# Softplus of a selective scan's steps: one function table, sums on TensorE, clamped integers in bf16, one store semaphore for each pair of buffers

## The chip, the core and the metric

The kernel runs on one core of a Trainium2 chip. The time is device microseconds for one execution. The kernel before takes 3646.77 us, the median of three runs (3645.39 to 3648.1). The work is spread over TensorE (PE in the profile), VectorE (DVE), ScalarE (ACT), GpSimd (POOL) and the DMA queues that SyncE (SP) issues to. The engines wait for each other through semaphores that the kernel sets by hand.

## The reference

Six layers follow each other on four sequences of 512 tokens of width 512: a quantized state-space layer, a cross-attention, a sparse mixture of experts, a self-attention, another cross-attention and another mixture. The change is in the first. What matters of it:

```python
dt8 = qa(dt_q @ dwq.T * (S_DTLN * dws), S_DT)      # round, clip to -128..127
dt = jax.nn.softplus(jnp.swapaxes(dt8, 1, 2) * S_DT + dt_bias[None, :, None])
u = u_q * S_U
A = -jnp.exp(A_log)
ys = ssm_scan(u, dt, A, B_q * S_B, C_q * S_C)      # needs dt and dt * u
```

So for each of 1024 channels and 4 x 512 tokens a product is rounded and clipped to an integer, scaled, a bias of the channel is added, and softplus of it, `dt`, and `dt * u` go to the scan.

## The kernel before

The kernel is a chain of sections, each ended by a barrier of all engines. The section here is `softplus` (L897 to L1007); ahead of it stands `x_proj`, behind it `scan`. It works on blocks of one sequence each (`NB` = 4, index `b`). A block is 8 tiles of 128 channels x 512 tokens, taken in pairs (`PAIRS` = 4, index `i`), so that an instruction mostly covers 128x1024 elements. The buffers `v` and `e` (f32) exist twice, for even and odd blocks, `w` once. The stages of a pair:

- products (L943, TensorE): two bf16 matmuls into PSUM `dps`, which has room for four pairs.
- rounding (L955, ScalarE): scale and add the constant MAGIC, which leaves an integer in the low bits; into `v`.
- clamping (L987, L988, VectorE): clip, then subtract MAGIC and multiply by the step, in place.
- bias (L965, ScalarE): one instruction for each tile, in place in `v`.
- Abs and Exp (L969, L972, ScalarE): e = exp(-|v|), into `e`.
- loss (L995, L996, VectorE): w = e - ((e + 1) - 1), what rounding loses of e when 1 is added.
- Ln (L977, ScalarE): e = ln(1 + e).
- steps (L1002, L1003, L1006, VectorE): w = e + w; v = max(v, 0) + w, which is dt; e = v * u.
- stores (L927, L929, SyncE): dt and dt * u to DRAM, two DMAs of 512 KB for a pair.

The order on each engine is that of its program. ScalarE goes through a block stage by stage: bias, Abs, Exp for the four pairs, then the rounding of the next block, then Ln. VectorE does four losses, clamps the next block, and then does four steps. A buffer `v` or `e` of a block may be written again when all eight stores of the block two before have landed; one semaphore for each half (`s_st[b % 2]`) counts them, and the first rounding of the block waits for it. Exp and Ln lie in different function tables, so the compiler puts a table load (ACT_TABLE_LOAD) ahead of each Exp stage and each Ln stage. SyncE fills `bc` at the head of the section with 32 broadcasts for the scan, and GpSimd works off a chain of small gathers and scatters (`add_cells`) beside all this. The section ends when the stores have landed and GpSimd is done.

Of the kernel before, what the change touches and what calls it, by code (L numbers as in the profile page):

```python
# [291 lines left out]
def mamba(nc, A, x_dram, xa, u, gate, owq, dtq, zero, rmw, soft, sgd, bcd, kv, gqk, ident, identb):  # L292
    with ExitStack() as ctx:
# [27 lines left out]
        softplus(nc, xa, u, dtq, dwq, dtb, kk, soft, bcd, rmw)  # L321
# [575 lines left out]
def softplus(nc, xa, u, dtq, dwq, dtb, kk, soft, bcd, rmw):  # L897
    with ExitStack() as ctx:
# [6 lines left out]
        dps = ctx.enter_context(nc.psum_tensor("sf_ps", [P, 4, 2, S], F32))  # L905
        bc = xa[:].rearrange("p j c -> p (j c)").bitcast(BF16).rearrange("p (m s) -> p m s", s=S)
        dtd, dud = soft
        with section(nc, "sf_mm", "sf_rnd", "sf_t", "sf_v", "sf_av", "sf_e", "sf_c", "sf_ln", "sf_dt", "sf_du", "sf_own",
                     "sf_bc", "sf_sum", "sf_st0", "sf_st1") as (
                block, s_mm, s_rnd, s_t, s_v, s_av, s_e, s_c, s_ln, s_dt, s_du, s_own, s_bc, s_sum, *s_st):  # L910
# [8 lines left out]
            @block.sync  # L919
            def _(sp):  # L920
                for m in range(2 * NS):
                    sp.dma_start(bc[:, m, :], bcd[m, 0:S].partition_broadcast(P)).then_inc(s_bc, 16)
                for b in range(NB):
                    for i in range(PAIRS):
                        n, k = b * PAIRS + i, b * CT + 2 * i
                        sp.wait_ge(s_dt, n + 1)
                        sp.dma_start(dtd[k:k + 2].rearrange("k p s -> p k s"), two(v, b, i)).then_inc(s_st[b % 2], 16)  # L927
                        sp.wait_ge(s_du, n + 1)
                        sp.dma_start(dud[k:k + 2].rearrange("k p s -> p k s"), two(e, b, i)).then_inc(s_st[b % 2], 16)  # L929
                sp.wait_ge(s_bc, 32 * NS)  # L930
                for s_half in s_st:
                    sp.wait_ge(s_half, 32 * PAIRS * (NB // 2))

            @block.tensor
            def _(pe):
                for b in range(NB):
                    for i in range(PAIRS):
                        n = b * PAIRS + i
                        if n >= 4:
                            pe.wait_ge(s_rnd, n - 3)  # L940
                        for h in range(2):
                            j = 2 * i + h
                            ins = pe.matmul(dps[:, n % 4, h, :], dwq[:, j * P:(j + 1) * P], dtq[:, b * S:(b + 1) * S],  # L943
                                            start=True, stop=True)
                        ins.then_inc(s_mm, 1)

            @block.scalar
            def _(act):
                def rounded(b):
                    for i in range(PAIRS):  # L950
                        n = b * PAIRS + i
                        act.wait_ge(s_mm, n + 1)
                        if b >= 2 and i == 0:
                            act.wait_ge(s_st[b % 2], 32 * PAIRS * (b // 2))
                        act.activation(two(v, b, i), dps[:, n % 4], ACT.Copy, scale=kk[:, W_DT:W_DT + 1],  # L955
                                       bias=MAGIC).then_inc(s_rnd, 1)

                rounded(0)
                for b in range(NB):
                    for i in range(PAIRS):  # L960
                        n = b * PAIRS + i
                        act.wait_ge(s_t, n + 1)
                        for h in range(2):
                            j = 2 * i + h
                            ins = act.activation(v[:, b % 2, j, :], v[:, b % 2, j, :], ACT.Identity, bias=dtb[:, j:j + 1])  # L965
                        ins.then_inc(s_v, 1)
# [13 lines left out]
            def _(dve):  # L980
                own = Order(dve, s_own)

                def clamped(b):
                    for i in range(PAIRS):
                        x = two(v, b, i)
                        dve.wait_ge(s_rnd, b * PAIRS + i + 1)
                        own.after(dve.tensor_scalar(x, x, MAGIC - 128.0, MAGIC + 127.0, ALU.max, ALU.min))  # L987
                        dve.tensor_scalar(x, x, MAGIC, S_DT, ALU.subtract, ALU.mult).then_inc(s_t, 1)  # L988

                clamped(0)  # L990
                for b in range(NB):
                    for i in range(PAIRS):
                        c = w[:, 2 * i:2 * i + 2, :]
                        dve.wait_ge(s_e, b * PAIRS + i + 1)
                        own.after(dve.tensor_scalar(c, two(e, b, i), 1.0, -1.0, ALU.add, ALU.add))  # L995
                        dve.tensor_tensor(c, two(e, b, i), c, ALU.subtract).then_inc(s_c, 1)  # L996
                    if b + 1 < NB:
                        clamped(b + 1)
                    for i in range(PAIRS):
                        n, c = b * PAIRS + i, w[:, 2 * i:2 * i + 2, :]  # L1000
                        dve.wait_ge(s_ln, n + 1)
                        own.after(dve.tensor_tensor(c, two(e, b, i), c, ALU.add))  # L1002
                        dve.scalar_tensor_tensor(out=two(v, b, i), in0=two(v, b, i), scalar=0.0, in1=c, op0=ALU.max,  # L1003
                                                 op1=ALU.add).then_inc(s_dt, 1)
                        dve.wait_ge(s_dt, n + 1)
                        dve.tensor_tensor(two(e, b, i), two(v, b, i), u[:, 2 * i:2 * i + 2, b * S:(b + 1) * S],  # L1006
                                          ALU.mult).then_inc(s_du, 1)  # L1007
# [1942 lines left out]
```

## Time and profile before

| | |
|---|---|
| median of 3 runs | 3646.77 us |
| profiled execution | 3662.09 us |
| its span, first to last instruction | 3660.3 us |
| TensorE, VectorE, ScalarE, GpSimd busy over the span | 88%, 66%, 48%, 33% |
| softplus, first product to VectorE's last operation | 266.64 to 387.39 us |
| table loads in softplus | 8, of 1283 ns each |

The numbers of the profile come from one execution with the profiler on; its own time is a little above the median of the runs. Busy times are shares of one engine, and a busy engine is only the bound where others wait for it. For a section this short the timeline says more than the busy share: start, length, and in brackets how long the engine had been idle before an instruction and what ended that. Matmuls overlap in the records, so their rate is read from their starts or from a sum over many. The granted clock of TensorE is a share of 2.4 GHz.

### The profile page before, as it was taken

The page shows a single profiled execution, that of the slowest core. Times are in us where ns is not written, and L with a number is a line of the kernel's source. Part 1 is how long each engine was busy: PE and PEld are TensorE (multiplying, and loading weights), DVE is VectorE, ACT ScalarE, POOL GpSimd, SP SyncE. Part 2 cuts the span into 40 slices and gives each one's busy share as a digit, 9 for nine tenths or more (in the row PEclk, how much of TensorE's full clock was granted, in tenths as well). Part 3 has the DMA queues.
Part 4 walks back from the last instruction along what each step waited for, and adds up shares of the span by engine and source line. Part 5 has one row for each costly group of instructions (what it writes and reads, how often), then busy time and mean ns, then how long its engine had stood idle before and what let it go on. Part 6 is the DMA issues. An engine that isn't in the chain of part 4 may idle for free. (4 is left out here: it accounts for less than half of the span.)

```text
span 3660.3 us, 34737 instructions
## 1 busy us (share of the span) xinstructions
PE 3219.4 (88%) x11045; PEld 1571.0 (43%) x11045; DVE 2431.8 (66%) x4472; ACT 1773.1 (48%) x3342; POOL 1203.4 (33%) x963
## 2 busy tenths in 40 slices
PE   3750699999999799999999999899899978999963
PEld 3330244444444345555455555344444444444432
DVE  8768899999999555555555555543421266999754
ACT  4748466666666334343434343344310125888621
POOL 0323699999999001010000000021388020000024
PEclk9975799999999899999999999999999997999977
DMA  7115425353432222222211111243622011000056
GB/s 258 48 60 166 149 93 147 100 138 101 124 112 75 99 74 67 69 78 66 70 52 52 61 55 52 95 139 123 231 106 98 0 64 58 1 1 1 1 162 212
DMA packets 201318, 334.67 MB, mean 91 GB/s; under 512 B 25648, under 2 KB 76208, under 8 KB 198064
## 3 DMA queue, kind: packets, MB, share of 16 engines
q1 hardware_dynamic: 187904, 298.69, 25.0%
q0 software_dynamic: 12208, 33.57, 3.3%
q8 instruction: 89, 1.46, 0.2%
q14 instruction: 93, 0.76, 0.1%
q10 hardware_dynamic: 1024, 0.20, 0.0%
HBM read 217.69 MB, written 114.69 MB: 91 GB/s over the span
## 5 line engine op out<-in xcount | busy, mean ns | idle before, releaser
L1282 POOL TENSOR_TENSOR sc_dBu<-sc_dtu,xa 128x1024 f32<-128x1024 f32 x256 | 540.0, 2131 | 42.1 <-DMA sc_dtu<-scan_dtu 32.9
L1192 PE MATMUL y_ps<-sc_g,ident 128*128 128x512 f32 x1024 | 476.0, 600 | 18.5 <-POOL sc_g L1270 11.6
L1306 DVE TENSOR_TENSOR_SCAN sc_dA<-sc_dA,sc_dBu 128x1024 f32<-128x1024 f32 x160 | 365.1, 2282 | 7.1 <-POOL sc_dBu L1282 7.1
L1565 ACT ACTIVATE c_p<-c_ps,c_sm 128x512 f32<-128x512 f32 x256 | 195.6, 774 | 352.9 <-DVE c_sm L1606 352.9
L1605 DVE TENSOR_REDUCE c_sm<-c_ps 128x4 f32<-128x2048 f32 x64 | 146.7, 2292 | 313.1 <-PE c_ps L1528 313.1
L1246 ACT ACTIVATE sc_dA<-sc_dt,a_neg 128x511 f32<-128x511 f32 x512 | 329.6, 676 | 11.4 <-DVE sc_g L1306 9.8
L1192 PEld LDWEIGHTS y_ps<-sc_g,ident 128*128 128x128 f32 x1024 | 190.0, 190 | 256.1 <-issue 169.2
L1598 DVE SCALAR_TENSOR_TENSOR xa<-c_ps,c_sm,xa 128x512 f32<-128x512 f32 x256 | 192.2, 751 | 146.9 <-PE c_ps L1518 133.3
L1518 PE MATMUL c_ps<-c_wo,c_oT 128*128 128x512 f32 x512 | 246.5, 605 | 2.3 <-DVE xa L1598 1.6
L1499 PE MATMUL c_ps<-u,c_wq 128*128 128x512 f32 x512 | 231.9, 596 | 4.5 <-DMA c_wq<-in_c_wq_dram 4.5
L1547 PE MATMUL c_ps<-c_pT,c_v 128*128 128x512 f32 x512 | 231.7, 595 | 2.8 <-DVE c_pT L1617 2.8
L1528 PE MATMUL c_ps<-c_kT,c_qT 128*128 128x512 f32 x512 | 230.2, 592 | 0.0
L1306 DVE TENSOR_TENSOR_SCAN sc_g<-sc_dA,sc_dBu 128x1024 f32<-128x1024 f32 x96 | 218.8, 2279 | 0.0
L1270 POOL TENSOR_TENSOR sc_g<-sc_g,xa 128x1024 f32<-128x1024 f32 x96 | 204.4, 2130 | 42.8 <-DVE sc_g L1306 42.6
L1485 POOL TENSOR_TENSOR e_d<-e_raw,e_wT 128x256 f32<-128x256 f32 x64 | 52.5, 858 | 473.6 <-DMA e_raw<-sparse_table 473.6
L1316 DVE TENSOR_TENSOR sc_g<-sc_dA,xa 128x1024 f32<-128x1024 f32 x160 | 196.0, 1225 | 16.3
L1750 POOL IOTA e_it<- 128x128 f32 x1 | 0.4, 353 | 597.0 <-POOLq L38 597.0
L2494 ACT ACTIVATE h_p<-h_ps,h_sm 128x496 f32<-128x496 f32 x256 | 170.0, 673 | 11.1 <-DVE h_sm L2526 10.5
L2634 POOL IOTA e_it<- 128x192 f32 x1 | 0.4, 365 | 517.2 <-POOLq L38 517.2
L2504 ACT ACTIVATE h_pT<-h_ps 128x1024 f32<-128x1024 f32 x128 | 131.0, 1024 | 71.4 <-PE h_ps L2422 71.4
L1572 ACT ACTIVATE c_pT<-c_ps 128x512 f32<-128x512 f32 x192 | 107.7, 595 | 117.1 <-PE c_ps L1537 117.1
L2412 PE MATMUL h_ps<-u,e_d 32*128 32x512 f32 x512 | 153.3, 686 | 10.0 <-ACT h_p L2496 7.2
(516 smaller groups left out, 6089.8 us busy)
## 6 DMA issues: line engine op xcount, KB each, us to landing
kv_w<-in_c_wkv_dram SPq DMA_DIRECT2D x32, 512.0 KB, 4.0
cross_keys<-kv_out SPq DMA_DIRECT2D x64, 256.0 KB, 2.0
cross_values<-kv_out SPq DMA_DIRECT2D x128, 128.0 KB, 1.9
c_kT<-cross_keys SPq DMA_DIRECT2D x64, 256.0 KB
c_rk<-cross_rk SPq DMA_DIRECT2D x64, 256.0 KB
c_v<-cross_values SPq DMA_DIRECT2D x64, 256.0 KB, 2.6
expert_rows<-e_yt SPq DMA_DIRECT2D x63, 256.0 KB, 2.0
xa<-scan_bc SPq DMA_DIRECT2D x48, 256.0 KB, 7.9
```

The lines of the kernel that those rows point to most:

```text
L1192: ins = pe.matmul(yps[:, k % 2, :], ident[:], g[:, c % GS, n, :], start=False, stop=(m == NCH - 1 and n == NG - 1))
L1246: ins = act.activation(dA[:, c % 2, n, 1:S], dt[:, k % DT, 1:S], ACT.Exp, scale=a_neg[:, k % CT, at:at + 1])
L1270: pool.tensor_tensor(g[:, c % GS], g[:, c % GS], bc[:, NS + m * NG:NS + (m + 1) * NG, :], ALU.mult).then_inc(s_gp, 1)
L1282: pool.tensor_tensor(dBu[:, c % 3], spread(dtu[:, k % DT, :], NG), bc[:, m * NG:(m + 1) * NG, :], ALU.mult).then_inc(s_dBu, 1)
L1306: dve.tensor_tensor_scan(to.rearrange("p n s -> p (n s)"), dA[:, c % 2].rearrange("p n s -> p (n s)"), dBu[:, c % 3].rearrange("p n s -> p ...
L1316: dve.tensor_tensor(g[:, c % GS], dA[:, c % 2], bc[:, NS + m * NG:NS + (m + 1) * NG, :], ALU.mult).then_inc(s_g, 1)
L1499: ins = pe.matmul(ps[:, QB, :], wq[:, h % 2, c, :], xT[:, c, b * S:(b + 1) * S], start=(c == 0), stop=(c == HC - 1))
L1518: pe.matmul(ps[:, YB + j % 2, :], oT[:, j * P:(j + 1) * P], wo[:, h % 2, :], start=True, stop=True).then_inc(s_y, 1)
L1528: ins = pe.matmul(ps[:, SB + j, :], qT[:, j * P:(j + 1) * P], kT[:, n % 2, :], start=True, stop=True)
L1547: ins = pe.matmul(ps[:, OB, :], v[:, n % 2, kt, :], pT[:, kt, :], start=(kt == 0), stop=(kt == TT - 1))
L1565: ins = act.activation(pr[:, j, :], ps[:, SB + j, :], ACT.Exp, scale=rq[:, j:j + 1], bias=bias[:, j:j + 1], accum_out=l[:, j:j + 1])
L1598: dve.scalar_tensor_tensor(out=xt, in0=ps[:, YB + j % 2, :], scalar=rl[:, j:j + 1], in1=xt, op0=ALU.mult, op1=ALU.add).then_inc(s_ye, 1)
```

## The change

- ScalarE loads one table that holds both Exp and Ln at the head of the section (`preload_act_table_set`).
- The clamp writes a new bf16 buffer `r`: the first operation subtracts MAGIC and clips at -128, the second clips at 127. The bias instruction reads `r` and multiplies by the step itself. Before the next block may write into `r`, its bias stage must be done (`s_v`).
- TensorE adds Ln and loss: for each tile two f32 matmuls against the identity into PSUM `lps`, which has room for two pairs. VectorE's first step operation goes away, and the next one reads `lps`. `dps` shrinks from four pairs to two.
- TensorE's order is products of the first block, then in turn products of block b + 1 and sums of block b (`logs`). The sums of a pair wait for loss, Ln, and for the step of the pair two before.
- VectorE does three steps of a block after the clamps, and the fourth in the next block, after two losses.
- The rounding of a pair waits for the two stores of that pair alone; eight semaphores instead of two.

```diff
--- before.py
+++ after.py
@@ -318,7 +318,7 @@
                 in_proj_conv(nc, A, xa, xq, wq, hs, u, gate, owq, dtq, dwq, xwq, sgd, rmw, cw, cb, mx, mxa, winv, wsc,
                              kk, identb)
             x_proj(nc, u, xwq, bct, dtq, lnw, kk, bcd, rmw, identb)
-        softplus(nc, xa, u, dtq, dwq, dtb, kk, soft, bcd, rmw)
+        softplus(nc, xa, u, dtq, dwq, dtb, kk, soft, bcd, rmw, ident)
         ssk = sb("c0_ssk", [P, S], F32)
         scan(nc, A, xa, u, gate, dsk, a_neg, soft, sgd, bcd, kv, ssk, ident)
         out_proj(nc, A, x_dram, xa, gate, owq, kk, ssk, kv[2], first_columns(u), gqk, ident)
@@ -894,7 +894,7 @@
 PAIRS = CT // 2
 
 
-def softplus(nc, xa, u, dtq, dwq, dtb, kk, soft, bcd, rmw):
+def softplus(nc, xa, u, dtq, dwq, dtb, kk, soft, bcd, rmw, ident):
     with ExitStack() as ctx:
         def sb(name, shape, dt=F32):
             return ctx.enter_context(nc.sbuf_tensor(name, shape, dt))
@@ -902,12 +902,14 @@
         v = sb("sf_v", [P, 2, CT, S])
         e = sb("sf_e", [P, 2, CT, S])
         w = sb("sf_w", [P, CT, S])
-        dps = ctx.enter_context(nc.psum_tensor("sf_ps", [P, 4, 2, S], F32))
+        r = sb("sf_r", [P, CT, S], BF16)
+        dps = ctx.enter_context(nc.psum_tensor("sf_ps", [P, 2, 2, S], F32))
+        lps = ctx.enter_context(nc.psum_tensor("sf_lps", [P, 2, 2, S], F32))
         bc = xa[:].rearrange("p j c -> p (j c)").bitcast(BF16).rearrange("p (m s) -> p m s", s=S)
         dtd, dud = soft
         with section(nc, "sf_mm", "sf_rnd", "sf_t", "sf_v", "sf_av", "sf_e", "sf_c", "sf_ln", "sf_dt", "sf_du", "sf_own",
-                     "sf_bc", "sf_sum", "sf_st0", "sf_st1") as (
-                block, s_mm, s_rnd, s_t, s_v, s_av, s_e, s_c, s_ln, s_dt, s_du, s_own, s_bc, s_sum, *s_st):
+                     "sf_bc", "sf_sum", "sf_add", *(f"sf_st{q}" for q in range(2 * PAIRS))) as (
+                block, s_mm, s_rnd, s_t, s_v, s_av, s_e, s_c, s_ln, s_dt, s_du, s_own, s_bc, s_sum, s_add, *s_st):
             @block.gpsimd
             def _(pool):
                 add_cells(pool, rmw, s_sum, CELL_STEPS[1], CELL_STEPS[2])
@@ -924,25 +926,44 @@
                     for i in range(PAIRS):
                         n, k = b * PAIRS + i, b * CT + 2 * i
                         sp.wait_ge(s_dt, n + 1)
-                        sp.dma_start(dtd[k:k + 2].rearrange("k p s -> p k s"), two(v, b, i)).then_inc(s_st[b % 2], 16)
+                        sp.dma_start(dtd[k:k + 2].rearrange("k p s -> p k s"), two(v, b, i)).then_inc(s_st[b % 2 * PAIRS + i], 16)
                         sp.wait_ge(s_du, n + 1)
-                        sp.dma_start(dud[k:k + 2].rearrange("k p s -> p k s"), two(e, b, i)).then_inc(s_st[b % 2], 16)
+                        sp.dma_start(dud[k:k + 2].rearrange("k p s -> p k s"), two(e, b, i)).then_inc(s_st[b % 2 * PAIRS + i], 16)
                 sp.wait_ge(s_bc, 32 * NS)
                 for s_half in s_st:
-                    sp.wait_ge(s_half, 32 * PAIRS * (NB // 2))
+                    sp.wait_ge(s_half, 32 * (NB // 2))
 
             @block.tensor
             def _(pe):
-                for b in range(NB):
+                def products(b):
                     for i in range(PAIRS):
                         n = b * PAIRS + i
-                        if n >= 4:
-                            pe.wait_ge(s_rnd, n - 3)
+                        if n >= 2:
+                            pe.wait_ge(s_rnd, n - 1)
                         for h in range(2):
                             j = 2 * i + h
-                            ins = pe.matmul(dps[:, n % 4, h, :], dwq[:, j * P:(j + 1) * P], dtq[:, b * S:(b + 1) * S],
+                            ins = pe.matmul(dps[:, n % 2, h, :], dwq[:, j * P:(j + 1) * P], dtq[:, b * S:(b + 1) * S],
                                             start=True, stop=True)
                         ins.then_inc(s_mm, 1)
+
+                def logs(b):
+                    for i in range(PAIRS):
+                        n = b * PAIRS + i
+                        if n >= 2:
+                            pe.wait_ge(s_dt, n - 1)
+                        pe.wait_ge(s_c, n + 1)
+                        pe.wait_ge(s_ln, n + 1)
+                        for h in range(2):
+                            j = 2 * i + h
+                            pe.matmul(lps[:, n % 2, h, :], ident[:], w[:, j, :], start=True, stop=False)
+                            ins = pe.matmul(lps[:, n % 2, h, :], ident[:], e[:, b % 2, j, :], start=False, stop=True)
+                        ins.then_inc(s_add, 1)
+
+                products(0)
+                for b in range(NB):
+                    if b + 1 < NB:
+                        products(b + 1)
+                    logs(b)
 
             @block.scalar
             def _(act):
@@ -950,11 +971,12 @@
                     for i in range(PAIRS):
                         n = b * PAIRS + i
                         act.wait_ge(s_mm, n + 1)
-                        if b >= 2 and i == 0:
-                            act.wait_ge(s_st[b % 2], 32 * PAIRS * (b // 2))
-                        act.activation(two(v, b, i), dps[:, n % 4], ACT.Copy, scale=kk[:, W_DT:W_DT + 1],
+                        if b >= 2:
+                            act.wait_ge(s_st[b % 2 * PAIRS + i], 32 * (b // 2))
+                        act.activation(two(v, b, i), dps[:, n % 2], ACT.Copy, scale=kk[:, W_DT:W_DT + 1],
                                        bias=MAGIC).then_inc(s_rnd, 1)
 
+                act.preload_act_table_set("natural_log_exp_and_others")
                 rounded(0)
                 for b in range(NB):
                     for i in range(PAIRS):
@@ -962,7 +984,7 @@
                         act.wait_ge(s_t, n + 1)
                         for h in range(2):
                             j = 2 * i + h
-                            ins = act.activation(v[:, b % 2, j, :], v[:, b % 2, j, :], ACT.Identity, bias=dtb[:, j:j + 1])
+                            ins = act.activation(v[:, b % 2, j, :], r[:, j, :], ACT.Identity, scale=S_DT, bias=dtb[:, j:j + 1])
                         ins.then_inc(s_v, 1)
                     for i in range(PAIRS):
                         act.wait_ge(s_v, b * PAIRS + i + 1)
@@ -982,29 +1004,41 @@
 
                 def clamped(b):
                     for i in range(PAIRS):
-                        x = two(v, b, i)
-                        dve.wait_ge(s_rnd, b * PAIRS + i + 1)
-                        own.after(dve.tensor_scalar(x, x, MAGIC - 128.0, MAGIC + 127.0, ALU.max, ALU.min))
-                        dve.tensor_scalar(x, x, MAGIC, S_DT, ALU.subtract, ALU.mult).then_inc(s_t, 1)
+                        n, x = b * PAIRS + i, r[:, 2 * i:2 * i + 2, :]
+                        dve.wait_ge(s_rnd, n + 1)
+                        if b:
+                            dve.wait_ge(s_v, n - PAIRS + 1)
+                        own.after(dve.tensor_scalar(x, two(v, b, i), MAGIC, -128.0, ALU.subtract, ALU.max))
+                        dve.tensor_scalar(x, x, 127.0, None, ALU.min).then_inc(s_t, 1)
+
+                def lost(b, i):
+                    c = w[:, 2 * i:2 * i + 2, :]
+                    dve.wait_ge(s_e, b * PAIRS + i + 1)
+                    if b:
+                        dve.wait_ge(s_add, (b - 1) * PAIRS + i + 1)
+                    own.after(dve.tensor_scalar(c, two(e, b, i), 1.0, -1.0, ALU.add, ALU.add))
+                    dve.tensor_tensor(c, two(e, b, i), c, ALU.subtract).then_inc(s_c, 1)
+
+                def stepped(b, i):
+                    n = b * PAIRS + i
+                    dve.wait_ge(s_add, n + 1)
+                    dve.scalar_tensor_tensor(out=two(v, b, i), in0=two(v, b, i), scalar=0.0, in1=lps[:, n % 2], op0=ALU.max,
+                                             op1=ALU.add).then_inc(s_dt, 1)
+                    dve.wait_ge(s_dt, n + 1)
+                    dve.tensor_tensor(two(e, b, i), two(v, b, i), u[:, 2 * i:2 * i + 2, b * S:(b + 1) * S],
+                                      ALU.mult).then_inc(s_du, 1)
 
                 clamped(0)
                 for b in range(NB):
                     for i in range(PAIRS):
-                        c = w[:, 2 * i:2 * i + 2, :]
-                        dve.wait_ge(s_e, b * PAIRS + i + 1)
-                        own.after(dve.tensor_scalar(c, two(e, b, i), 1.0, -1.0, ALU.add, ALU.add))
-                        dve.tensor_tensor(c, two(e, b, i), c, ALU.subtract).then_inc(s_c, 1)
+                        if b and i == PAIRS // 2:
+                            stepped(b - 1, PAIRS - 1)
+                        lost(b, i)
                     if b + 1 < NB:
                         clamped(b + 1)
-                    for i in range(PAIRS):
-                        n, c = b * PAIRS + i, w[:, 2 * i:2 * i + 2, :]
-                        dve.wait_ge(s_ln, n + 1)
-                        own.after(dve.tensor_tensor(c, two(e, b, i), c, ALU.add))
-                        dve.scalar_tensor_tensor(out=two(v, b, i), in0=two(v, b, i), scalar=0.0, in1=c, op0=ALU.max,
-                                                 op1=ALU.add).then_inc(s_dt, 1)
-                        dve.wait_ge(s_dt, n + 1)
-                        dve.tensor_tensor(two(e, b, i), two(v, b, i), u[:, 2 * i:2 * i + 2, b * S:(b + 1) * S],
-                                          ALU.mult).then_inc(s_du, 1)
+                    for i in range(PAIRS - 1):
+                        stepped(b, i)
+                stepped(NB - 1, PAIRS - 1)
 
 
 GS = 3
```

VectorE in the second block, before: the last step of the first block (L1003, L1006), then losses.

```order
L1003 SCALAR_TENSOR_TENSOR sf_v<-sf_v,sf_w 128x1024
L1006 TENSOR_TENSOR sf_e<-sf_v,u 128x1024
L995 TENSOR_SCALAR sf_w<-sf_e 128x1024
L996 TENSOR_TENSOR sf_w<-sf_e,sf_w 128x1024
L995 TENSOR_SCALAR sf_w<-sf_e 128x1024
L996 TENSOR_TENSOR sf_w<-sf_e,sf_w 128x1024
L995 TENSOR_SCALAR sf_w<-sf_e 128x1024
L996 TENSOR_TENSOR sf_w<-sf_e,sf_w 128x1024
```

The same place now: two losses (L1019, L1020), the fourth step of the first block (L1025, L1028), the third loss.

```order
L1019 TENSOR_SCALAR sf_w<-sf_e 128x1024
L1020 TENSOR_TENSOR sf_w<-sf_e,sf_w 128x1024
L1019 TENSOR_SCALAR sf_w<-sf_e 128x1024
L1020 TENSOR_TENSOR sf_w<-sf_e,sf_w 128x1024
L1025 SCALAR_TENSOR_TENSOR sf_v<-sf_v,sf_lps 128x1024
L1028 TENSOR_TENSOR sf_e<-sf_v,u 128x1024
L1019 TENSOR_SCALAR sf_w<-sf_e 128x1024
L1020 TENSOR_TENSOR sf_w<-sf_e,sf_w 128x1024
```

The last step of a block, and with it its last store, has moved behind two losses of the next block, and each step is two operations instead of three.

ScalarE from the first Exp stage to the second, before:

```order
L972 ACT_TABLE_LOAD
L972 ACTIVATE sf_e<-sf_e 128x1024 x4
L955 ACTIVATE sf_v<-sf_ps,kk 128x1024 x4
L977 ACT_TABLE_LOAD
L977 ACTIVATE sf_e<-sf_e 128x1024 x4
L965 ACTIVATE sf_v<-sf_v,dtb 128x512 x8
L969 ACTIVATE sf_e<-sf_v 128x1024 x4
L972 ACT_TABLE_LOAD
```

The same stages now (L994 Exp, L976 rounding, L999 Ln, L987 bias, L991 Abs):

```order
L994 ACTIVATE sf_e<-sf_e 128x1024 x4
L976 ACTIVATE sf_v<-sf_ps,kk 128x1024 x4
L999 ACTIVATE sf_e<-sf_e 128x1024 x4
L987 ACTIVATE sf_v<-sf_r,dtb 128x512 x8
L991 ACTIVATE sf_e<-sf_v 128x1024 x4
```

The order of the stages is the same; the loads between them are gone, and the bias reads `sf_r`. The only load left in the section stands at its head, and the one that stood ahead of the scan's first Exp is gone too.

## Rows read from the trace of the kernel before

**Rows 1.** Windows, softplus: length, busy PE, PEld, DVE, ACT, POOL, clock, DMA share, GB/s.

```profile
266.64:387.39 120.75, 14.04 (x32) 3.06 (x32) 107.77 (x112) 92.88 (x104) 37.24 (x36) 0.51 0.51 167
```

**Rows 2.** Timeline of VectorE in softplus: start us, us, engine, line, operation, idle before.

```profile
282.88 0.69 DVE L995 TENSOR_SCALAR sf_w<-sf_e 128x1024 f32<-128x1024 f32 x1 [8.58 <-ACT sf_e L972]
...
310.31 0.69 DVE L995 TENSOR_SCALAR sf_w<-sf_e 128x1024 f32<-128x1024 f32 x1
311.03 1.22 DVE L996 TENSOR_TENSOR sf_w<-sf_e,sf_w 128x1024 f32<-128x1024 f32 x1
312.17 0.69 DVE L995 TENSOR_SCALAR sf_w<-sf_e 128x1024 f32<-128x1024 f32 x1
...
365.23 0.69 DVE L995 TENSOR_SCALAR sf_w<-sf_e 128x1024 f32<-128x1024 f32 x1
...
384.90 1.23 DVE L1003 SCALAR_TENSOR_TENSOR sf_v<-sf_v,sf_w 128x1024 f32<-128x1024 f32 x1
386.16 1.23 DVE L1006 TENSOR_TENSOR sf_e<-sf_v,u 128x1024 f32<-128x1024 f32 x1
```

**Rows 3.** Timeline of ScalarE in softplus, same columns, stages merged.

```profile
267.69 4.13 ACT L955 ACTIVATE sf_v<-sf_ps,kk 128x1024 f32<-128x1024 f32 x4 [3.24 <-PE sf_ps L943]
...
280.50 1.28 ACT L972 ACT_TABLE_LOAD   x1
281.79 3.90 ACT L972 ACTIVATE sf_e<-sf_e 128x1024 f32<-128x1024 f32 x4
285.59 4.10 ACT L955 ACTIVATE sf_v<-sf_ps,kk 128x1024 f32<-128x1024 f32 x4
289.71 1.28 ACT L977 ACT_TABLE_LOAD   x1
291.01 3.90 ACT L977 ACTIVATE sf_e<-sf_e 128x1024 f32<-128x1024 f32 x4
294.81 5.00 ACT L965 ACTIVATE sf_v<-sf_v,dtb 128x512 f32<-128x512 f32 x8
299.72 3.88 ACT L969 ACTIVATE sf_e<-sf_v 128x1024 f32<-128x1024 f32 x4
...
313.40 4.12 ACT L955 ACTIVATE sf_v<-sf_ps,kk 128x1024 f32<-128x1024 f32 x4 [4.60 <-DMA scan_dtu<-sf_e]
```

**Rows 4.** Groups of VectorE lines: count, busy us, mean ns, idle before.

```profile
L1598 DVE SCALAR_TENSOR_TENSOR xa<-c_ps,c_sm,xa 128x512 f32<-128x512 f32 x256 | 192.2, 751 | 146.9 <-PE c_ps L1518 133.3
...
L1958 DVE SCALAR_TENSOR_TENSOR xa<-e_gy,e_rw,xa 128x512 f32<-128x512 f32 x32 | 24.0, 751 | 12.9 <-DMA e_gy<-expert_rows,e_row 10.7 <-DVE xa L1958 0.3
...
L782 DVE TENSOR_SCALAR gate<-gate 128x2048 bf16<-128x2048 bf16 x8 | 5.6, 694 | 0.3
...
L582 DVE TENSOR_SCALAR xb_m<-xb_m 128x512 bf16<-128x512 bf16 x16 | 4.7, 297 | 0.6
```

**Rows 5.** TensorE's f32 matmuls: timeline and windows at the scan's head, groups.

```profile
402.42 3.78 PE L1192 MATMUL y_ps<-sc_g,ident 128*128 128x512 f32 x4 [6.74 <-DVE sc_g L1316]
406.00 2.84 PE L1170 MATMUL kv_ps<-kv_cT,kv_w 128*128 128x512 f32 x4
...
406.00:407.00 1.00, 1.00 (x3) 0.48 (x2) 0.97 (x2) 0.00 (x0) 1.00 (x2) 0.50 0.36 133
408.00:409.00 1.00, 1.00 (x3) 0.39 (x3) 1.00 (x2) 0.96 (x3) 1.00 (x1) 1.00 0.00 0
...
L1192 PE MATMUL y_ps<-sc_g,ident 128*128 128x512 f32 x4 | 3.8, 1102 | 6.7 <-DVE sc_g L1316 6.7
...
L1192 PEld LDWEIGHTS y_ps<-sc_g,ident 128*128 128x128 f32 x1024 | 190.0, 190 | 256.1 <-issue 169.2
...
L1528 PE MATMUL c_ps<-c_kT,c_qT 128*128 128x512 f32 x512 | 230.2, 592 | 0.0
```

**Rows 6.** Timeline of the DMA issues, pair 3 of block 0.

```profile
310.42 0.36 SPq L929 DMA_DIRECT2D scan_dtu<-sf_e  x1
```

**Rows 7.** Timeline of POOL, its last issue in softplus.

```profile
361.99 1.66 POOL L622 DMA_INDIRECT sparse_table<-new,locu  x1 [0.28 <-POOL new L620]
```

## The prediction

> **What bounds the kernel now.** I read the windows of the section first, then the timelines of VectorE, ScalarE and TensorE in it, then groups of lines elsewhere for prices that the section doesn't show. The change touches one section, softplus, which runs from 266.64 to 387.39 us. VectorE is busy for 107.8 us of its 120.75, ScalarE for 92.9, TensorE for 14.0 [rows 1]. The reader is to see in VectorE's timeline that after its first loss at 282.88 no operation waits: the next block's begins at 310.31, the last one's at 365.23, so a steady block takes 54.92 / 2 = 27.46 us, and the section's end is VectorE's last operation, 386.16 + 1.23 = 387.39 [rows 2]. ScalarE waits for stores before the rounding of blocks 2 and 3 (4.6 us in the row shown) and is otherwise full up to the last block, with a table load ahead of each Exp and each Ln stage, eight in all [rows 3]. So VectorE bounds it, and ScalarE is the next in line: its block without loads is 3.80 (Exp) + 4.00 (rounding) + 3.80 (Ln) + 4.91 (bias) + 3.80 (Abs) = 20.3 us, from start to start of the stages [rows 3]; rounding (4.10) and Abs (3.88) are counted less about 0.08, by which a stage starts before the end of the one ahead where no load stands between (281.79 + 3.90 against 285.59 shows 0.10).
>
> **The change part by part.** VectorE works in pairs of tiles, four to a block, four blocks.
>
> Clamping: one 128x1024 operation from f32 into bf16, and one from bf16 into bf16. The first reads f32 as now and has a constant for its second operand, like the first operation of a loss; I give it that one's pitch, wait included, 311.03 - 310.31 = 0.72 us [rows 2]. The second isn't in this size in the trace. The same kind took 297 ns on 512 and 694 ns on 2048 elements [rows 4]; on the straight line between them 1024 elements take 0.43 us, and as an operation that needn't wait starts 0.08 us before the one ahead has ended (311.03 + 1.22 against 312.17), its pitch is 0.35. From the other side, if it runs at the pace of the two-operand subtraction, it is 312.17 - 311.03 = 1.14. I take 0.35, since its row is of the same kind. A clamped pair costs 1.07; now it is 0.72 and, for the second in f32, 0.69 - 0.08: 1.33.
>
> The loss (two operations) stays: 312.17 - 310.31 = 1.86 us.
>
> Adding Ln and loss: 1.26 us of VectorE goes away in each of 16 pairs. The max-and-add that is left reads one operand from PSUM; it took 386.16 - 384.90 = 1.26 and the product with u 1.23 - 0.08 = 1.15 [rows 2], 2.41 together. An operation of that form took 751 ns with a PSUM operand and 751 ns with all in SBUF [rows 4], so I add nothing. The Trainium skill (VectorE: DVE Perf Modes, The TRN2 errata) gives 120 fixed cycles for a PSUM source and 58 for an SBUF one. By that each would be about 0.06 us dearer, an estimate, and the sum some 0.5 us smaller; the two rows at 751 speak against it.
>
> So VectorE's steady block is 4 x (1.07 + 1.86 + 2.41) = 21.4 us, 6.1 less than now.
>
> TensorE gets four f32 128x512 matmuls a pair against the identity. What its clock is then matters. At the head of the scan, where it had long been idle, the granted clock is 0.50, that is 1.2 GHz, and four such matmuls take 406.00 - 402.42 = 3.6 us; the clock is at 1.00 in the row from 408, after some 5.5 us of uninterrupted work [rows 5]. At 2.4 GHz 512 of them took 230.2 us, 1.8 for four [rows 5]. The section as a whole had a mean of 0.51 [rows 1], so every block's sums start at the low level. I take 3.6, 2.5, 1.8 and 1.8 us for the four pairs of a block, all 3.6 as the upper bound, and 1.8 as the lower. A block's sums are then 10 us in a TensorE that has about 23 idle.
>
> ScalarE loses seven table loads of 1.28 us, and the eighth becomes one at the head. That one lies beside the wait for the first product (266.64 to 267.69) and can stick out by 0.2. The load in front of the scan goes as well, but ScalarE then waited for a DMA, so it gives nothing. The Trainium skill (ScalarE: Activation LUTs, What ACT_TABLE_LOAD costs) puts a switch at 1283 ns of load and about 1380 ns of drain. The trace has the 1283 ns but not the drain: rounding ends at 289.69, Ln starts at 291.01, 1.32 us for all [rows 3]. By the page ScalarE's seven switches would be 18.6 us, an estimate, by the rows 9.2; neither is the gain, since VectorE was the bound. Elsewhere Exp now comes from another set of functions. Exp and Ln, each from its own set, took the same 3.90 us for four [rows 3], so I price that at nothing.
>
> Two PSUM pairs instead of four: the third product of a block waits for the first rounding (1.1 us), runs 0.9 to 1.0 at the low clock, and is 0.15 late. I count 0.15 a block on ScalarE.
>
> Stores: rounding pair i of block b+2 waits for the stores of pair i of block b alone. But pair 3 is now stepped late, in the next block after two losses. Between the issue of the store of u's product and ScalarE's start there were 313.40 - 310.42 = 3.0 us [rows 3, 6], and the issue follows the operation's end at once. Behind the waiting rounding stand Ln, bias, Abs and Exp of ScalarE. That wait takes the place of the old one and is what is late next.
>
> **The sum**, by the first Exp of each block (E, when VectorE can start its losses; 282.88 now). First: the load in front of it is gone, so Exp starts at 280.50 + 0.15 + 0.2, and E0 = 281.9. That is 1.0 earlier.
> Block 0 to 1: no buffer has been stored yet, and ScalarE bounds: 20.3 + 0.15 = 20.5, against 27.4 now. E1 = 302.4, 6.9 more.
> Blocks 1 to 2 and 2 to 3: two losses 3.73, then stepped pair 3 of the block before, 2.41 + 0.08 to its end; + 3.0 store = E + 9.2 for the last rounding. Then 1.0 + Ln 3.8 + bias 4.9 + Abs 3.8 + first Exp 1.1 = 14.6. Together 23.8, above VectorE's 21.4, against 27.46. E3 = 350.0, and 2 x 3.65 = 7.3 more.
> Last: four losses and five stepped pairs, 7.46 + 12.05 + 0.1 = 19.6, against 387.39 - 365.23 = 22.16. VectorE ends at 369.6, 2.6 more.
> 1.0 + 6.9 + 7.3 + 2.6 = 17.8 us. The stores and the barrier behind move along unchanged. POOL's chain of table updates, which hid under the section, has its last issue at 361.99, ended at 363.65 [rows 7]; with 3.0 us to land, as for a store, it is done by 367, and the section's last store lands at 372.6, so it stays hidden by over 5 us. The profiled execution took 3662.09 us, so 3644.3 for a profiled one; it lies 15.3 above the median of the runs, and I carry the difference over: 3646.8 - 17.8 = 3629.0.
>
> **Rivals.**
> TensorE becomes the bound, and the kernel slower. With x us for the four sums of a pair, the way round is three sums, a stepped pair, two losses, another stepped pair, store, rounding and Ln: 3x + 2.4 + 3.7 + 2.5 + 3.0 + 1.1 + 1.0 = 3x + 13.7. That is 24.5 at 3.6, and passes the present 27.46 at x = 4.6. The group of the scan's first sums shows 1102 ns for each and the group of their weight loads 190 [rows 5]; if neither overlapped here, x would be 4 x 1.29 = 5.2: a block of 29.3, steps that wait in the last block too (3x + two steps behind the first Ln), and VectorE's end near 393, 5 to 6 later than now: 3652. For it: a low clock at every start, and four waits a pair. Against: four started within 3.6 us there, for the records overlap, and the clock rose in work like this. 5%.
> The clock stays at 1.2 GHz all through: 24.5 for the two blocks, 1.4 more, and in the last block each sum of 3.6 waits for the step two before it, some 1.5 more; VectorE ends near 372.5, 3632. Or the second clamp costs 1.14: then a clamped pair (1.86) comes slower than its bias (1.23), which holds ScalarE up by about 1 us in every block; near 373.5, 3633. Together 15%.
> The store wait doesn't bite (landing sooner or ScalarE gets slack): VectorE's 21.4 bounds two blocks, which gives 4.8 more, 3624. The 3.0 us measured for a store speaks against it. 8%.
> The semaphore of each pair doesn't do what it says, since the last pair's store is the late one whichever semaphore carries it: all four roundings then wait rather than one, 3.1 more in two blocks, 3635. For it: pair 3 is the only late one. Against: pairs 0 to 2 are stored some 10 us earlier, so three roundings can pass. 7%.
> The forecast as summed, 3626 to 3631.5: 65%.
>
> **How the numbers follow.** The range 3624 to 3636 takes in all but the rival on TensorE and a remainder for prices in other sections that no row shows. About 0.2%, 7.3 us, is what a measurement of this kernel can tell from no change; faster means under 3639.5. Only TensorE's rival, in part, and that remainder reach past it: faster 0.93, same 0.05, slower 0.02.
>
> **What would show it.** In the changed profile: one table load at the head of the section and none before the scan; VectorE's end near 369.6; starts of the first loss of the blocks 20.5, 23.8 and 23.8 apart; ScalarE waiting about 3 us for the store of pair 3 before the last rounding of blocks 2 and 3, and not before the other three; bf16 clamps of 0.43 us; sums of 3.6 us in the first pair of a block and 1.8 in the last; max-and-add at 1.23. It is wrong if ScalarE waits for TensorE's sums anywhere but there, if blocks are 21 or 28 apart, or if the scan or the attention stages change by more than a few us.

## The result, and the profile after

The changed kernel takes 3638.38 us (median of 15 runs, 3631.75 to 3643.37), the kernel before 3646.38 (15 runs): a ratio of 0.998, 95% interval 0.9973 to 0.9988, or 8 us less. Forecast were 3629.0, 17.8 less, with a range of 3624 to 3636; the measured time lies 2.4 us above it. The direction was right, the gain less than half of what was forecast.

| from the first product on, us | before | forecast | after |
|---|---|---|---|
| first loss, block 0 | 16.2 | 15.3 | 15.3 |
| block 0 to 1 | 27.4 | 20.5 | 22.9 |
| blocks 1 to 2, 2 to 3 | 27.5, 27.5 | 23.8, 23.8 | 26.8, 27.0 |
| last block to VectorE's end | 22.2 | 19.6 | 21.4 |
| sum | 120.75 | 103 | 113.4 |

The section is 7.35 us shorter in these two traces, and that is the gain in the main. The two profiled executions differ by 25 us, of which 3.2 lie ahead of the section and 12.3 between 2384 and 3072 us of the trace before, in code that the change doesn't touch: the same stretch took 687.7 us before, 675.4 after, and 693.1 in another execution of the changed kernel. So single executions can't be compared by their spans here, only stretch by stretch.

VectorE in the changed kernel, the timeline of softplus (start us, us, engine, line, operation, idle before and what ended it):

```profile
278.69 0.69 DVE L1019 TENSOR_SCALAR sf_w<-sf_e 128x1024 f32<-128x1024 f32 x1 [8.32 <-ACT sf_e L994]
...
301.60 0.73 DVE L1019 TENSOR_SCALAR sf_w<-sf_e 128x1024 f32<-128x1024 f32 x1
...
315.40 0.43 DVE L1012 TENSOR_SCALAR sf_r<-sf_r 128x1024 bf16<-128x1024 bf16 x1
319.10 1.22 DVE L1025 SCALAR_TENSOR_TENSOR sf_v<-sf_v,sf_lps 128x1024 f32<-128x1024 f32 x1 [3.28 <-PE sf_lps L959]
320.36 1.23 DVE L1028 TENSOR_TENSOR sf_e<-sf_v,u 128x1024 f32<-128x1024 f32 x1
322.54 1.22 DVE L1025 SCALAR_TENSOR_TENSOR sf_v<-sf_v,sf_lps 128x1024 f32<-128x1024 f32 x1 [0.95 <-PE sf_lps L959]
323.79 1.23 DVE L1028 TENSOR_TENSOR sf_e<-sf_v,u 128x1024 f32<-128x1024 f32 x1
325.97 1.22 DVE L1025 SCALAR_TENSOR_TENSOR sf_v<-sf_v,sf_lps 128x1024 f32<-128x1024 f32 x1 [0.95 <-PE sf_lps L959]
327.23 1.23 DVE L1028 TENSOR_TENSOR sf_e<-sf_v,u 128x1024 f32<-128x1024 f32 x1
328.37 0.74 DVE L1019 TENSOR_SCALAR sf_w<-sf_e 128x1024 f32<-128x1024 f32 x1
...
375.59 1.23 DVE L1028 TENSOR_TENSOR sf_e<-sf_v,u 128x1024 f32<-128x1024 f32 x1
```

Where VectorE never waited before [rows 2], it now waits for TensorE ahead of its steps: 3.28 us, then 0.95 and 0.95 in the block shown, 16.0 us in 11 places in the whole section. Steps come 322.54 - 319.10 = 3.44 us apart, and not 2.41. The prices of its own operations are as forecast: bf16 clamp 0.43, max-and-add from PSUM 1.22.

ScalarE in the changed kernel, timeline of the rounding of block 2:

```profile
303.06 3.12 ACT L976 ACTIVATE sf_v<-sf_ps,kk 128x1024 f32<-128x1024 f32 x3 [1.07 <-PE sf_ps L945]
310.87 1.11 ACT L976 ACTIVATE sf_v<-sf_ps,kk 128x1024 f32<-128x1024 f32 x1 [4.69 <-DMA scan_dtu<-sf_e]
311.88 3.88 ACT L999 ACTIVATE sf_e<-sf_e 128x1024 f32<-128x1024 f32 x4
```

Three roundings pass and the fourth waits for a store, 310.87 - 301.60 = 9.3 us after the first loss (9.2 forecast). It answers to the row of 313.40 in [rows 3]. The 1.07 us ahead of the first three is new: the products of the next block now stand behind the sums on TensorE. The fourth rounding waits for the store all the same, so it costs nothing here.

TensorE in the changed kernel, timeline of the sums of block 1 up to the start of its third pair, each row one tile's loss or Ln, and the group of all losses:

```profile
313.08 2.04 PE L958 MATMUL sf_lps<-sf_w,ident 128*128 128x512 f32 x2 [7.24 <-ACT sf_e L999]
314.91 1.91 PE L959 MATMUL sf_lps<-sf_e,ident 128*128 128x512 f32 x2
316.62 1.59 PE L958 MATMUL sf_lps<-sf_w,ident 128*128 128x512 f32 x2
318.04 1.02 PE L959 MATMUL sf_lps<-sf_e,ident 128*128 128x512 f32 x2
318.90 1.02 PE L958 MATMUL sf_lps<-sf_w,ident 128*128 128x512 f32 x2
...
322.33 1.02 PE L958 MATMUL sf_lps<-sf_w,ident 128*128 128x512 f32 x2
```

```profile
L958 PE MATMUL sf_lps<-sf_w,ident 128*128 128x512 f32 x64 | 38.2, 682 | 18.9 <-ACT sf_e L999 18.9
```

Here is the error. The program calls L958 32 times, the group has 64. Every f32 matmul runs as two instructions (the rows' x2), one bf16 matmul as one. A pair's sums are eight instructions: 322.33 - 318.90 = 3.43 us at 2.4 GHz. The first pair of the block, which starts at half the clock, takes 5.8 up to the next pair's start (313.08 to 318.90) and 6.0 up to VectorE's step (319.10).

### The profile page after: what moved, and what is told of

Its sections match the earlier page's. It is cut to its first block and busy times, and to the rows that moved or that the text cites. A ratio compares the mean times of both kernels' runs of the same rounds, so it can differ in the third digit from the quotient of the medians.

```text
span 3635.1 us, 35018 instructions
## 1 busy us (share of the span) xinstructions
PE 3275.7 (90%) x11173; PEld 1598.0 (44%) x11173; DVE 2409.2 (66%) x4456; ACT 1762.1 (48%) x3334; POOL 1204.2 (33%) x963
## 5 line engine op out<-in xcount | busy, mean ns | idle before, releaser
L1280 ACT ACTIVATE sc_dA<-sc_dt,a_neg 128x511 f32<-128x511 f32 x512 | 329.6, 676 | 12.3 <-DVE sc_g L1340 9.8
L1562 PE MATMUL c_ps<-c_kT,c_qT 128*128 128x512 f32 x512 | 230.2, 592 | 0.0
L2456 PEld LDWEIGHTS h_ps<-ident,h_p 128*128 128x128 f32 x1024 | 117.2, 148 | 105.0 <-issue 76.3
```

The lines of the kernel that those rows point to most:

```text
L1280: ins = act.activation(dA[:, c % 2, n, 1:S], dt[:, k % DT, 1:S], ACT.Exp, scale=a_neg[:, k % CT, at:at + 1])
L1562: ins = pe.matmul(ps[:, SB + j, :], qT[:, j * P:(j + 1) * P], kT[:, n % 2, :], start=True, stop=True)
```

## Experiments

Theory A: TensorE's sums take 3.4 us a pair and 5 to 6 for the first, and the way round of a block is two losses, late step, store, rounding and Ln (9.3 + 1.0 + 1.1 us), then the sums of three pairs (6.0 + 3.4 + 3.4) and a step (2.4): 26.6, measured 26.8 and 27.0. Rivals stand in the expectations. "Section" is the time from the first product to VectorE's last operation, read from each trace; "blocks" are the distances between the first losses of blocks 0 to 1, 1 to 2 and 2 to 3; ratios are of the whole kernel, against the kernel before on the same chip, with their 95% intervals. Each section comes from one execution. The changed kernel's own three are 113.4 to 114.57, so about 1 us is what such a comparison can tell. The ratios don't separate all cases: those of the changed kernel and of the experiments on the clock, on the bf16 loss alone and on the order of steps overlap. What each of them did is read from the section.

**The changed kernel as base.** No edit.

> The changed kernel again, on the chip of the others, as their base. Its section (first product to VectorE's last operation) took 113.4 us in its trace, 120.75 before. Both theories expect about 113.4 and some 8 us less than before in all.

> The changed kernel once more, as the base of this call: section 113.4 to 114.3, about 7 us less than before in all.

Sections 114.25 and 114.57 us, blocks 23.6, 27.1, 27.2 in both; ratios 0.9984 (0.9972 to 0.9996) and 0.9981 (0.9972 to 0.999). Both fit within 1 us.

**Fewer passes on TensorE.** The loss goes out as bf16 (its f32 intermediate stays in a small buffer). The line that matters; the rest of the edit makes the two buffers.

```diff
-                            pe.matmul(lps[:, n % 2, h, :], ident[:], w[:, j, :], start=True, stop=False)
+                            pe.matmul(lps[:, n % 2, h, :], identb[:], wb[:, j, :], start=True, stop=False)
```

> The changed kernel with the loss stored as bf16 and added through the bf16 identity, so three quarters of the passes on TensorE. Theory A (an f32 128x512 matmul is two instructions on TensorE of 0.43 us each at 2.4 GHz, so a pair's sums take 3.4 us and not 1.8, more than VectorE's step of 2.4): a pair's sums fall to 6 instructions, 2.6 us, VectorE hardly waits for them, blocks fall from 26.8 to 23.9 us, the section to about 103 us, 10 less than the changed kernel. Theory B (the store of the late fourth pair bounds the blocks, and TensorE only fills the gap): blocks stay at 26 to 27, section within 2 us of 113.

Section 102.5, blocks 20.5, 23.8, 23.8; ratio 0.996 (0.9945 to 0.9975). TensorE's timeline in it:

```profile
317.04 0.38 PE L959 MATMUL sf_lps<-sf_wb,identb 128*128 128x512 bf16 x1
317.25 1.02 PE L960 MATMUL sf_lps<-sf_e,ident 128*128 128x512 f32 x2
318.11 0.38 PE L959 MATMUL sf_lps<-sf_wb,identb 128*128 128x512 bf16 x1
318.33 1.02 PE L960 MATMUL sf_lps<-sf_e,ident 128*128 128x512 f32 x2
319.19 0.38 PE L959 MATMUL sf_lps<-sf_wb,identb 128*128 128x512 bf16 x1
```

A bf16 matmul takes 0.21 us of TensorE, an f32 one of the same size 0.86, four times as much: 2.15 us a pair, even less than the 2.6 I expected (at the low clock the first pair takes 4.2). B falls. With this TensorE the section has the very blocks that the prediction laid out (20.5, 23.8, 23.8, and 19.5 for the last), and ScalarE waits 3.17 us for the store of the fourth pair, so its other terms held. The next section began 6.35 us after VectorE's end, 4.05 in the changed kernel. No run shows the cause of these 2.3 us.

**The clock.** Extra bf16 matmuls fill TensorE's gap ahead of the sums; their result is overwritten.

```diff
+                        if i == 0 and b:
+                            for _ in range(30 if b < NB - 1 else 10):
+                                pe.matmul(lps[:, n % 2, 0, :], dwq[:, 0:P], dtq[:, 0:S], start=True, stop=True)
```

> The changed kernel with 30 (10 in the last block) extra bf16 matmuls on TensorE ahead of the sums of blocks 1 to 3, whose result is overwritten, in time in which TensorE is idle. Theory A (the first pair's sums take 6.0 us and not 3.4 because the granted clock has fallen to 0.50 in the gap): first pairs at 3.4, blocks 1 and 2 at 24.5 instead of 27.1, the last 1.6 shorter, section about 107.5. Theory B (the first pair is slow for its semaphores and weight loads): first pairs stay at 6.0, section at 114 or a little more.

Section 108.6, blocks 23.7, 24.4, 24.5; ratio 0.9974 (0.9962 to 0.9986). Windows of 305.9 to 313.0 and of the first sums, first of the changed kernel, then of this one (length, busy TensorE, PEld, VectorE, ScalarE, GpSimd, granted clock, DMA share, GB/s):

```profile
305.90:313.00 7.10, 0.00 (x0) 0.00 (x0) 6.96 (x9) 2.41 (x4) 3.38 (x4) 0.61 0.42 149
313.08:318.90 5.82, 5.82 (x8) 2.52 (x9) 2.64 (x6) 5.82 (x9) 2.63 (x4) 0.60 0.03 1
```

```profile
305.90:313.00 7.10, 6.70 (x31) 2.85 (x31) 7.00 (x7) 2.43 (x3) 3.10 (x4) 1.00 0.41 149
313.08:318.90 5.82, 5.08 (x14) 2.20 (x13) 4.69 (x10) 5.82 (x8) 2.93 (x3) 1.00 0.03 1
```

With the gap filled the clock is 1.00 when the sums start. The second window holds some of the extra matmuls too, so the pair itself is read from TensorE's timeline in this run, first rows of the first and of the second pair, in block 1 and in the last block:

```profile
314.63 1.10 PE L961 MATMUL sf_lps<-sf_w,ident 128*128 128x512 f32 x2 [0.74 <-ACT sf_e L1002]
...
318.14 1.02 PE L961 MATMUL sf_lps<-sf_w,ident 128*128 128x512 f32 x2
...
355.36 1.10 PE L961 MATMUL sf_lps<-sf_w,ident 128*128 128x512 f32 x2
...
358.87 1.02 PE L961 MATMUL sf_lps<-sf_w,ident 128*128 128x512 f32 x2
```

The first pair takes 318.14 - 314.63 = 3.51 us instead of 5.8. The sums wait for the same semaphores and load the same weights as before, so it was the clock; blocks 1 to 2 and 2 to 3 are 2.3 and 2.6 us shorter. The last block gained 0.7 and not 1.6, and the section is 1 us longer than expected. In the whole kernel this gain doesn't show: the ratio's interval overlaps that of the changed kernel.

**The store wait.** Rounding of a block waits for all stores again.

```diff
-                        if b >= 2:
-                            act.wait_ge(s_st[b % 2 * PAIRS + i], 32 * (b // 2))
+                        if b >= 2 and i == 0:
+                            for s_pair in s_st[b % 2 * PAIRS:(b % 2 + 1) * PAIRS]:
+                                act.wait_ge(s_pair, 32 * (b // 2))
```

> The changed kernel, but the first rounding of a block waits for all stores of the block two before, as in the kernel before. Theory A (blocks 1 and 2 are a chain: two losses, late step, store 3.0 us, rounding, Ln, sums of the first three pairs): three roundings that lay ahead of the store now lie behind it, 3.1 us more in each of two blocks, periods of about 30, section about 120 against 113.4 to 114.3 of the changed kernel. Theory B (TensorE alone bounds, the store wait has slack): no change.

Section 121.6, blocks 23.8, 30.5, 30.7; ratio 0.9996 (0.9986 to 1.0005). ScalarE's timeline in it:

```profile
314.95 4.36 ACT L977 ACTIVATE sf_v<-sf_ps,kk 128x1024 f32<-128x1024 f32 x4 [9.75 <-DMA scan_dtu<-sf_e]
```

All four roundings now stand behind the store. With the late step in place, the semaphores of each pair are worth 7 us of the section, as much as the whole change gained; without them it would have gained nothing (the interval of the ratio contains 1).

**Sums back on VectorE.** `logs` is left out; `stepped` adds on VectorE, four steps in one piece. The lines that matter:

```diff
-                    dve.wait_ge(s_add, n + 1)
+                    dve.wait_ge(s_ln, n + 1)
+                    own.after(dve.tensor_tensor(c, two(e, b, i), c, ALU.add))
```

> The changed kernel with the sum of Ln and loss back on VectorE (and its four steps in one piece, as before); one table, bf16 clamps and the eight semaphores stay. Both theories: VectorE never waits, block 4 x (1.07 + 1.86 + 3.67) = 26.4 us, section about 116.4, 4.4 less than before and 3 more than the changed kernel. If TensorE's sums had brought nothing at all (theory C), it would equal the changed kernel.

Section 116.25, blocks 26.4 each; ratio 0.9994 (0.9982 to 1.0005). So the sums on TensorE together with the late step gained 2 to 3 us, not the 5 a block that leave VectorE. This run differs from the changed kernel in both; the next one tells them apart.

**Steps ahead of the losses.** The late step of the changed kernel is moved back in front of the next block (and the call behind the loops goes).

```diff
-                        if b and i == PAIRS // 2:
-                            stepped(b - 1, PAIRS - 1)
-                    for i in range(PAIRS - 1):
+                    for i in range(PAIRS):
                         stepped(b, i)
```

> The changed kernel, all f32 sums on TensorE, but all four steps of a block ahead of the next block's losses. Theory A: VectorE waits for all four pairs' sums (6.0 + 3 x 3.4 us) and then does the step, so blocks 1 and 2 are 24 to 24.5, the first 26 instead of 23.6, section 110.5 to 111.5 against 113.4 to 114.3. Theory B (a late step costs nothing, since VectorE has something to do while TensorE sums): section as the changed kernel or longer.

Section 111.65, blocks 27.1, 24.1, 24.0; ratio 0.996 (0.9945 to 0.9975). The first block was 1 us longer than expected. The late step, placed to keep VectorE busy, cost more through the store behind it than it saved: here the last rounding of block 2 waits 1.94 us for its store and not 4.69. Against the run before this one, whose order of steps is the same, the sums on TensorE alone are worth 116.25 - 111.65 = 4.6 us.

**Table alone**, on the kernel before.

```diff
+                act.preload_act_table_set("natural_log_exp_and_others")
                 rounded(0)
```

> The kernel before with the one table load at the head and nothing else. Both theories: VectorE is the bound and never waits but for the first Exp, so only the one load ahead of it goes: section 119.5 against 120.75, 1.3 us less. If table loads were a cost on the path (theory C), 10 us less.

Section 119.5, ratio 0.9996 (0.9987 to 1.0005). ScalarE's timeline:

```profile
308.22 4.12 ACT L955 ACTIVATE sf_v<-sf_ps,kk 128x1024 f32<-128x1024 f32 x4 [7.48 <-DMA scan_dtu<-sf_e]
```

The time of the removed loads reappears as a longer wait for the store, 7.48 us instead of 4.60 [rows 3]. In the ratio, 1.25 us can't be told from nothing.

**Clamps alone**, on the kernel before: the new `clamped` and the bias line of the change.

> The kernel before with only the bf16 clamps. VectorE is the bound there, and a clamped pair costs 1.07 instead of 1.33 us: 1.04 us less in each of four blocks, section 116.6 against 120.75. A rival: the bf16 operations slow other work on VectorE or GpSimd, then less than 3 us.

Section 117.5, 3.3 less; ratio 0.9989 (0.9979 to 0.9998). A steady block is 26.34, 1.1 less, as expected; the first loss is no earlier, since ScalarE sets it, and that is the missing one of four.

**Both: bf16 loss and steps ahead of the losses.** The edits of "Fewer passes on TensorE" and "Steps ahead of the losses" together.

> As e1_w_bf16, and all four steps of a block ahead of the next block's losses, so that the fourth store is issued earlier. Theory A: with sums of 2.6 us the fourth can follow at once; blocks of 21.4 us after a first of 22.6, section about 98 us, 15 less than the changed kernel, where GpSimd's chain of table updates (which ended 97 us after the first product) comes near to bounding the end. Theory B: the store no longer holds the rounding, so it would gain here even though e1_w_bf16 didn't.

Section 97.35, blocks 22.0, 21.35, 21.3; ratio 0.9954 (0.9936 to 0.9971). VectorE waits for nothing to speak of, its block is the 21.4 of the prediction. But the next section began at 107.9 and not at 101.4. Timeline of GpSimd, and of VectorE behind the section:

```profile
361.75 0.97 POOL L617 DMA_INDIRECT old<-sparse_table,locu  x1 [3.50 <-DMA sparse_table<-new,locu]
364.61 0.20 POOL L620 TENSOR_TENSOR new<-old,tot 128x8 f32<-128x8 f32 x1 [1.89 <-DMA old<-sparse_table,locu]
365.08 0.98 POOL L622 DMA_INDIRECT sparse_table<-new,locu  x1 [0.28 <-POOL new L620]
```

```profile
370.31 0.16 DVE L1078 MEMSET kv_hot<- 128x127 f32 x1 [10.53 <-DVEq L38]
```

VectorE is idle for 10.5 us while GpSimd's chain runs to 366.06. The chain had 12 steps as before, but was at its end 103.6 us after the first product instead of 97.0. In the changed kernel it ended after 97.2, in its two repeats after 98.1 and 96.0.

**And two table updates moved ahead.**

```diff
-CELL_STEPS = (14, 20, ST)
+CELL_STEPS = (14, 22, ST)
```

> As e6_best, and two of GpSimd's 12 table updates of this section are done in the section ahead (22 instead of 20 before this one), where GpSimd was done 12 us early. Theory A (in e6_best the section ends with GpSimd's chain: its last issue ended 103.6 us after the first product, VectorE 97.35, and the next section began at 107.9): chain over by 91, next section's first VectorE operation at 101.5 after the first product, 6.4 less, the section ahead unchanged; in all about 24 us less than before. Theory B (the end was set by barrier or stores): still 107 to 108.

> The fastest so far beside the changed kernel: next section begins 102.8 us after the first product, 15 us earlier than in the changed kernel (117.4 to 118.3); in all 15 us less than it and 22 less than before, with both intervals apart.

Section 97.95 and 97.97, next section at 102.8 both times; ratios 0.995 (0.9937 to 0.9964) and 0.9948 (0.9935 to 0.9962). On the chip of the second the median is 3628.91 against 3638.89 of the changed kernel and 3646.26 of the kernel before: it beats both. The gain of 17 to 18 us is less than the 21.9 by which the next section comes earlier. The section ahead pays for its two updates with 1 us at most: from its first product to that of softplus it took 47.2 and 46.8 us in these two traces, 46.0 to 47.0 in the twelve others with 20 updates ahead. The other 3 to 4 us may be the spread of 5 to 23 runs; no run settles it. The 15 us against the changed kernel that I had written down were 10.

## Why the prediction was wrong

The step that failed is the price of a pair's sums: "TensorE gets four f32 128x512 matmuls a pair", then "four such matmuls take 406.00 - 402.42 = 3.6 us" and "At 2.4 GHz 512 of them took 230.2 us, 1.8 for four". The two rows are read rightly, but they count instructions, not calls, and a call with f32 operands is two of them. The sums of a pair are 3.43 us at 2.4 GHz, and 5.2 to 6.1 for the first of a block. This could be read off the rows: L1192 stands in [rows 5] with x1024, while its loop makes 512 calls, L1528 with x512 for 256 calls, and the bf16 products stand in [rows 1] with x32 for 32 calls.

A second size was off the other way. The course of the four pairs, 3.6, 2.5, 1.8 and 1.8 us, would be 7.2, 5.0, 3.6 and 3.6 when doubled, and by the prediction's formula a block of 29.5 us, more than before. Measured were 5.8, 3.4 and 3.4, and 26.8: the granted clock was 0.50 up to 317.5 and 1.00 from 318 on, so it rose within the first pair. The right count alone would have missed on the other side.

By steps:

- Start and table: 1.0 us forecast, 1.0 found. That table loads weren't on the path held (1.25 alone).
- Block 0 to 1: 20.5 forecast, 22.9 found. ScalarE was done; VectorE's steps waited for the sums.
- Blocks 1 to 3: the store wait came at 9.3 us as forecast (9.2). Behind it I had ScalarE's 14.6 us; TensorE's way, 2.1 + 6.0 + 3.4 + 3.4 and a step, measured 17.5 and 17.8, was 2.9 and 3.2 longer.
- Last block: 19.6 forecast, 21.4 found, the same cause (0.74 and 0.95 of waits for sums).
- The rival "TensorE becomes the bound" was the right one. Its own formula, 3x + 13.7, gives 24.0 for x = 3.43, and 26.6 with 6.0 for the first. I gave it 5% because I tied it to the records' lengths, and priced it 14 us too dear. The rival "the clock stays at 1.2 GHz", 3632 and inside the range, rested on x = 3.6 as the upper bound for a pair, which was half of what the low clock makes (the first four of eight instructions of block 1 alone took 3.5).
- The rival on the semaphores fell: three roundings pass (303.06, x3), and that is worth 7 us.
- The late step: seen as "what is late next", but not asked whether the other order were better. With fast sums it costs 5 us (102.5 against 97.35), with slow ones 3.
- GpSimd's chain stayed hidden in the changed kernel with over 10 us to spare (over 5 forecast). It bounded the section of 97.35, in a trace where it ended 103.6 us after the first product.

## What to carry to other kernels

Before a price per instruction is multiplied with a count from the code, compare the code's count with the trace's for the same line; where they differ by a factor, as for f32 on TensorE here, the price of a call is that factor times an instruction's. When work moves to an engine that waits between its pieces, price the first piece at the clock which that engine has after the gap. And where a step is placed late to fill a wait, follow its store to who waits for that buffer.

## What the runs showed of the hardware

- An f32 128x512 matmul against the identity is two instructions 0.43 us apart at 2.4 GHz, 0.86 for a call; in bf16 it is one of 0.21.
- In the last block of the changed kernel TensorE had been idle for 2.24 us when its sums began, and the granted clock, 1.00 before and in the gap, was 0.50 from 359 to 362 (first pair 5.2 us). With ten bf16 matmuls in that gap the first pair took 3.51. Ahead of blocks 1 and 2 the gaps were 7.2 us and the first pairs 5.8 and 6.1, so the short gap cost nearly as much as the long ones.
- GpSimd's chain of 12 small gathers and scatters ended between 89.6 us (all stores of a block behind one wait) and 103.6 us (the fastest order, and as well with the sums on VectorE) after the first product. The wait between a scatter and the next gather was 1.39 us at its shortest, 3.50 ahead of the last step in the fastest order, and 7.0 to 7.7 after the first scatter of the section. What sets it isn't shown: both kernels with 103.6 differ much in how dense their stores are.
